# Gate and up products of the experts as three fp32r products, with operands split ahead

## The reference, cut to what matters

```python
h = 512; I = 256; E = 32; TOP_K = 6
def expert_step(acc, inp):
    gu, dn, c = inp
    g = xf @ gu[:I].T
    u = xf @ gu[I:].T
    o = jax.nn.silu(g) * u @ dn.T
    return (acc + c[:, None] * o, None)
routed, _ = jax.lax.scan(expert_step, jnp.zeros_like(xf), (experts_gate_up, experts_down, combine.T))
sh = jax.nn.silu(xf @ shared_gate_w.T) * (xf @ shared_up_w.T)
return (routed + sh @ shared_down_w.T).reshape(b, s, h)
```

## Time and profile before

| | us |
|---|---|
| median of three runs | 1537.28 |
| the profiled execution | 1538.13 |
| its span, first to last instruction | 1536.2 |
| attention stages and feed-forward | about 0 to 1180 |
| routing and shared expert | about 1180 to 1242 |
| loop over 42 expert blocks | about 1249 to 1513 |
| last adds, sums and stores | 1513 to 1536 |
| mean granted TensorE clock | 0.979 |

### The profile page before, as it was taken

How to read it: one execution, slowest core, us unless ns; L and a number is a source line. 1 busy time by engine, 2 the same in 40 slices (tenths; PEclk the granted TensorE clock), 3 DMA queues, 4 the chain that set the end, 5 groups by cost and what they waited for, 6 DMA issues and landing times. The chain is left out here.

```text
span 1536.2 us, 23747 instructions
## 1 busy us (share of the span) xinstructions
PE 1464.4 (95%) x8826; PEld 1191.7 (78%) x8826; DVE 844.1 (55%) x2161; ACT 549.2 (36%) x1022; POOL 565.4 (37%) x276
## 2 busy tenths in 40 slices
PE   5999999999999999999999999788998989999994
PEld 4999999989999999899989999636665445555552
DVE  6455555544586755488655578739402634444442
ACT  3344345344354354443444533522211012222331
POOL 5006006006366604374811554526400124444442
PEclk9999999999999999999999999989997999999997
DMA  5102003013003013002112200350004659999999
GB/s 197 63 4 90 5 4 121 4 62 94 26 5 97 3 71 118 28 4 65 33 48 92 78 1 1 148 249 1 1 0 158 229 179 333 350 331 341 332 338 301
DMA packets 63976, 176.97 MB, mean 115 GB/s; under 512 B 15110, under 2 KB 32006, under 8 KB 54028
## 3 DMA queue, kind: packets, MB, share of 16 engines
q1 hardware_dynamic: 53708, 151.57, 27.7%
q0 software_dynamic: 10176, 24.12, 6.4%
HBM read 156.00 MB, written 19.66 MB: 114 GB/s over the span
## 5 line engine op out<-in xcount | busy, mean ns | idle before, releaser
L65 PE MATMUL ps_x<-wkv_hi,c_hi 128*128 128x256 f32 (+1 forms) x832 | 241.2, 290 | 0.0
L67 PE MATMUL ps_x<-wkv_hi,c_lo 128*128 128x256 f32 (+1 forms) x832 | 234.2, 282 | 0.0
L66 PE MATMUL ps_x<-wkv_lo,c_hi 128*128 128x256 f32 (+1 forms) x832 | 234.2, 281 | 0.0
L294 POOL TENSOR_TENSOR c_hi<-c_raw,ones 128x1608 fp32r<-128x1608 f32 x31 | 90.1, 2905 | 344.8 <-DMA c_raw<-ctxT 344.8
L769 DVE TENSOR_TENSOR pT<-ps_x,pT 128x512 fp32r<-128x512 f32 (+1 forms) x224 | 145.1, 648 | 123.3 <-ACT pT L617 120.6
L65 PE MATMUL ps_x<-c_hi,wkv_hi 128*128 128x402 f32 x512 | 195.7, 382 | 2.9 <-POOL c_lo L297 2.3
L617 ACT CAST pT<-ps_x 128x512 fp32r<-128x512 f32 (+1 forms) x224 | 124.5, 556 | 167.4 <-PE ps_x L472 164.4
L67 PE MATMUL ps_x<-c_hi,wkv_lo 128*128 128x402 f32 x512 | 177.9, 347 | 0.0
L66 PE MATMUL ps_x<-c_lo,wkv_hi 128*128 128x402 f32 x512 | 177.8, 347 | 0.0
L65 PEld LDWEIGHTS ps_x<-wkv_hi,c_hi 128*128 128x128 f32 (+1 forms) x832 | 153.5, 184 | 17.0 <-issue 17.0
L598 ACT CAST vv<-ps_x 128x512 fp32r<-128x512 f32 (+1 forms) x112 | 62.1, 555 | 278.5 <-PE ps_x L67 278.5
(11 more groups left out here) (314 smaller groups left out, 2685.6 us busy)
## 6 DMA issues: line engine op xcount, KB each, us to landing
e_w_gu<-w_gu SPq DMA_DIRECT2D x49, 1024.0 KB, 7.9
c_raw<-ctxT SPq DMA_DIRECT2D x32, 804.0 KB, 5.0
e_w_dn<-w_dn SPq DMA_DIRECT2D x48, 512.0 KB, 5.6
x_tok<-slabs SPq DMA_DIRECT2D x13, 1024.0 KB, 4.8
spare<-slabs SPq DMA_DIRECT2D x8, 1024.0 KB, 11.1
h_late<-slabs SPq DMA_DIRECT2D x4, 1024.0 KB, 16.6
e_mix<-shared SPq DMA_DIRECT2D x2, 1536.0 KB, 8.5
wkv_raw<-w_qkv SPq DMA_DIRECT2D x2, 1024.0 KB, 12.3
```

The costliest lines, as they stand in the source:

```text
L65: nc.tensor.matmul(out, a_hi, b_hi, start=start, stop=False)
L66: nc.tensor.matmul(out, a_hi, b_lo, start=False, stop=False)
L67: return nc.tensor.matmul(out, a_lo, b_hi, start=False, stop=stop)
L294: nc.gpsimd.tensor_tensor(c_hi[:, :, chunk(c)], c_raw[:, :, chunk(c)], ones[:, 0:1].unsqueeze(2).to_broadcast([P, KD, CW]), ALU.mult).then ...
```

## The change

The weights of gate and up are loaded into `gu_raw` as before. ScalarE now rounds them to fp32r (`split_high`, 2048 numbers in each partition, into a ring of three), three blocks ahead. VectorE subtracts to get the low part of three of the four slices (`split_low`, 1536 numbers), GpSimd that of the fourth (512 numbers), both two blocks ahead and in place, over `gu_raw`. The turned block is split too: ScalarE's copy writes its high part and VectorE's `turned_low` (512 numbers from PSUM) the low part. `gate_up` becomes four calls of mm3, twelve fp32r matmuls. `turned` now waits until gate_up of two blocks before is done, as its ring has two places instead of six. `pick_slots` makes its table in one instruction with broadcasts instead of four, into a ring of two. Ahead of the loop, the wait for the tables and the reading of the loop count are moved ahead of shared_down(1), the turns of the first two blocks lie between the shared expert's down products, VectorE makes the first table for the loop before hidden(0), and the first splits lie around them. Two buffers of the shared expert share space with the third place of the high ring.

```diff
-        w_gu = sb("e_w_gu", [P, U, KD, 2 * I])
+        gu_raw = sb("e_gu_raw", [P, U, KD, 2 * I])
+        gu_lo = nc.alloc_sbuf_tensor_at("e_gu_lo", [P, U, KD, 2 * I], F32R, offset=nc.sbuf_base - 4 * U * KD * 2 * I)
+        gu_hi = sb("e_gu_hi", [P, 3, KD, 2 * I], F32R)
+        gu_hi_2 = nc.sbuf_base - 4 * KD * 2 * I
+        assert 4 * T * 4 <= 4 * KD * 2 * I
...
-        pick = sb("e_pick", [P, U, TT, P], F32R)
+        pick = sb("e_pick", [P, 2, TT, P], F32R)
...
-        xT = sb("e_xT", [P, U, D])
+        xT_hi, xT_lo = (sb(f"e_xT_{n}", [P, 2, D], F32R) for n in ("hi", "lo"))
...
-        s_sg, s_t1, s_hid = sb("r_sg", [P, 2, T]), sb("r_t1", [P, 2, T]), sb("r_hid", [P, 2, 2, T])
+        s_sg, s_t1 = (nc.alloc_sbuf_tensor_at(f"r_{n}", [P, 2, T], F32, offset=gu_hi_2 + 8 * T * i) for i, n in enumerate(("sg", "t1")))
+        s_hid = sb("r_hid", [P, 2, 2, T])
...
-        xT_full, xT_done = sem("e_xT_full"), sem("e_xT_done")
+        xT_full, xT_hi_done, xT_lo_done = sem("e_xT_full"), sem("e_xT_hi_done"), sem("e_xT_lo_done")
+        gu_hi_done, gu_lo_done, gu_lo3_done = sem("e_gu_hi_done"), sem("e_gu_lo_done"), sem("e_gu_lo3_done")
...
                     wait_turn(sp, gu_full, nth(i, r, plus=1 - U))
-                sp.dma_start(w_gu[:, r % U], a["w_gu"][e]).then_inc(gu_loaded[r % U], 16)
+                sp.dma_start(gu_raw[:, r % U], a["w_gu"][e]).then_inc(gu_loaded[r % U], 16)
             def down(i, r, first=False):
...
+            def split_low(i, r):
+                wait_turn(pool, gu_hi_done, nth(i, r, plus=1))
+                nc.gpsimd.tensor_tensor(gu_lo[:, r % U, 3], gu_raw[:, r % U, 3], f32(gu_hi[:, r % 3, 3]), ALU.subtract).then_inc(gu_lo3_done, 1)
+
...
             for r in range(AHEAD):
                 gather(0, r)
+                if r >= AHEAD - 2:
+                    split_low(0, r + 2 - AHEAD)
...
             with pool.Fori(0, turns(pool)) as i:
                 for r in range(U):
                     gather(i, r + AHEAD)
+                    split_low(i, r + 2)
                     scatter(i, r)
...
-                if not isinstance(i, int) or r >= U:
-                    dve.wait_ge(info_full, nth(i, r, plus=1 - U))
+                if not isinstance(i, int) or r >= 2:
+                    dve.wait_ge(info_full, nth(i, r, plus=-1))
...
-                for t in range(TT):
-                    ins = nc.vector.tensor_scalar(pick[:, b, t], slot[:, 0:P], rel[:, b, t:t + 1], None, ALU.is_equal)
-                ins.then_inc(pick_done, 1)
+                nc.vector.tensor_tensor(pick[:, r % 2], slot[:, 0:P].unsqueeze(1).to_broadcast([P, TT, P]),
+                                        rel[:, b].unsqueeze(2).to_broadcast([P, TT, P]), ALU.is_equal).then_inc(pick_done, 1)
+
+            def split_low(i, r):
+                dve.wait_ge(gu_hi_done, nth(i, r, plus=1))
+                nc.vector.tensor_tensor(gu_lo[:, r % U, 0:3], gu_raw[:, r % U, 0:3], f32(gu_hi[:, r % 3, 0:3]), ALU.subtract).then_inc(gu_lo_done, 1)
+
+            def turned_low(i, r):
+                dve.wait_ge(xT_hi_done, nth(i, r, plus=1))
+                nc.vector.tensor_tensor(xT_lo[:, r % 2], ps[:, XT], f32(xT_hi[:, r % 2]), ALU.subtract).then_inc(xT_lo_done, 1)
             def rows_in(i, r):
...
             for r in range(AHEAD):
...
+                else:
+                    split_low(0, 0)
                 rows_in(0, r)
...
                     shared_hidden(1 + r // 2)
+            split_low(0, 1)
             for t in range(TT):
...
+                if t in (1, 2):
+                    turned_low(0, t - 1)
+            pick_slots(0, AHEAD)
             hidden(0, 0)
-            pick_slots(0, AHEAD)
             with dve.Fori(0, turns(dve)) as i:
                 for r in range(U):
                     rows_in(i, r + AHEAD)
+                    split_low(i, r + 2)
+                    turned_low(i, r + 2)
...
                     hidden(i, r + 1)
             for t in range(TT):
...
         def _(act):
             def turned(i, r):
...
-                nc.scalar.copy(xT[:, r % U], ps[:, XT]).then_inc(xT_done, 1)
+                if not isinstance(i, int) or r >= 2:
+                    act.wait_ge(gu_full, nth(i, r, plus=-1))
+                nc.scalar.copy(xT_hi[:, r % 2], ps[:, XT]).then_inc(xT_hi_done, 1)
+
+            def split_high(i, r):
+                act.wait_ge(gu_loaded[r % U], landed(i, r))
+                if not isinstance(i, int) or r >= 3:
+                    act.wait_ge(gu_full, nth(i, r, plus=-2))
+                nc.scalar.copy(gu_hi[:, r % 3], gu_raw[:, r % U]).then_inc(gu_hi_done, 1)
             def gates(i, r):
...
+            for r in range(3):
+                if r == 2:
+                    act.wait_ge(s_hid_done, 4)
+                split_high(0, r)
             turned(0, 0)
             turned(0, 1)
             gates(0, 0)
...
                 for r in range(U):
                     turned(i, r + 2)
                     hidden_turned(i, r)
+                    split_high(i, r + 3)
                     gates(i, r + 1)
...
                 for t in range(TT):
-                    ins = nc.tensor.matmul(ps[:, INFO, 0:NF], pick[:, b, t], facts[:, b, t], start=(t == 0), stop=(t == TT - 1))
+                    ins = nc.tensor.matmul(ps[:, INFO, 0:NF], pick[:, r % 2, t], facts[:, b, t], start=(t == 0), stop=(t == TT - 1))
...
             def turn(i, r):
...
-                    pe.wait_ge(xT_done, nth(i, r))
+                    pe.wait_ge(xT_lo_done, nth(i, r))
...
             def gate_up(i, r):
...
-                pe.wait_ge(gu_loaded[b], landed(i, r))
-                pe.wait_ge(xT_done, nth(i, r, plus=1))
+                pe.wait_ge(gu_lo3_done, nth(i, r, plus=1))
+                pe.wait_ge(gu_lo_done, nth(i, r, plus=1))
+                pe.wait_ge(xT_lo_done, nth(i, r, plus=1))
...
-                    ins = nc.tensor.matmul(ps[:, GU], xT[:, b, P * g:P * g + P], w_gu[:, b, g], start=(g == 0), stop=(g == KD - 1))
+                    c = slice(P * g, P * g + P)
+                    ins = mm3(nc, ps[:, GU], xT_hi[:, r % 2, c], xT_lo[:, r % 2, c], gu_hi[:, r % 3, g], gu_lo[:, b, g],
+                              g == 0, g == KD - 1)
...
             def turn_hidden(i, r):
...
                 look_up(0, r)
             shared_down(0)
             look_up(0, AHEAD - 1)
-            for t in range(1, TT):
-                shared_down(t)
+            pe.wait_ge(tables_done, 2)
+            n = turns(pe)
+            shared_down(1)
             turn(0, 0)
+            shared_down(2)
             turn(0, 1)
+            shared_down(3)
...
-            pe.wait_ge(tables_done, 2)
-            n = turns(pe)
             with pe.Fori(0, n) as i:
                 for r in range(U):
                     look_up(i, r + AHEAD)
```

## The result

The changed kernel takes 1514.55 us (median of 4 runs, 1512.40 to 1515.61); the kernel before took 1537.74 us beside it (4 runs). The ratio is 0.9848, 95% interval 0.9836 to 0.9860. The profiled execution took 1515.2 us with a span of 1513.1 us, against a span of 1536.2 us before: 23.1 us less.

What follows compares the result with a forecast made beforehand. TensorE was taken to bound the loop at 6.23 us per block, the DMA engines close behind. Entry 4.9 us plus 41 x (6.23 - 5.95) = 11.5 us gave 16.4 us: 1521 us from the median of 1537.28, range 1504 to 1541 us.

Steps and rivals of the forecast that it cites:

- the case that made the forecast: Loop: DMA engines or a light lock set a block of 5.8 to 6.2 us, 1515 to 1532 us; chance 0.54.
- Products: gate_up on TensorE: twelve fp32r matmuls, 2.76 to 2.84 us, replace 3.44 us; TensorE's block falls to 5.55 to 5.63 us.
- ScalarE: Loop: one added rounding of 1.90 us brings ScalarE to 3.8 us per block, hidden with 0.2 us to spare.
- VectorE: Loop: with split_low, turned_low and the one-instruction table, VectorE needs 5.4 us per block beside TensorE's 5.6.
- the lock: Loop: VectorE waits a whole 1.27 us GpSimd instruction per block, block 6.67 us, 1550 us; chance 0.15.
- GpSimd: Loop: with a 1.27 us split added, scatter, gather and split take 4.8 to 5.5 us per block and fit, barely.
- DMA pace: Loop: the DMA engines need 5.95 us to move a block's 2.1 MB, taken for all blocks.
- the signs that I named for this pace: Loop profile: gate_up waits for a split while ScalarE waits for weights, landings grow past 12 us, rate over 360 GB/s.
- Entry: Ahead of the loop: gate_up(2) waits for GpSimd's third split until 1255.4 us, saving 4.9 us; bounds 2 and 8.5 us.
- End: Behind the last block: unused loads queue ahead of the final reads of the sums, so the end follows DMA pace.
- TensorE's pace: Loop: TensorE sets a block of 5.60 us and the DMA engines have room, 31 us gained, 1507 us; chance 0.25.

Runs made afterwards that it cites:

- two products: The changed kernel with the product of low turned block by high weights left out of gate_up, all splits still made: 1512.07 us (1 run).
- three ahead: The changed kernel with GpSimd's split made three blocks ahead instead of two, one more split at the entry: 1526.20 us.
- the operand from PSUM: The changed kernel with VectorE's split in the loop taking its first input from PSUM, so one SBUF input instead of two: 1539.67 us.
- two slices: The changed kernel with GpSimd splitting two of the four slices and VectorE the other two: 1537.21 us (1 run).
- single products: Gate and up from one product of rounded weights by rounded turned block, no low parts made by any engine: 1502.59 us.
- the vector splits: The changed kernel with VectorE making the low part of all four slices and GpSimd none: 1506.58 us; once more, 1507.00 us.

## Why the prediction was right, and where it was off

The time lay in the range, and it moved the way that was forecast; the gain was 22.7 us from the median where 16.3 were forecast. Part of that is luck. The loop gained 20.9 us where 11.5 were forecast, and entry and end gave 1.5 and 1.2 us less than forecast. Its block of 5.70 us lies outside the 5.8 to 6.2 us of the case that made the forecast, and the cause was not the one named. By its own steps:

- **Products.** 12 x 0.23 us, and the free block at the entry is 5.59 us: inside 5.55 to 5.63. Right, and the removed cost was all there to be had.
- **ScalarE.** Hidden: it never appears in front of TensorE.
- **VectorE.** 5.4 us of work per block were forecast; it is busy 33.68 of 40 us, or 4.8 us per block of 5.70, the single terms as taken (1.76, 0.68, 0.69 us). It met the lock after all: lightly in the changed kernel (a mean of 1.82 instead of 1.76 us for its split), and by 0.6 to 1.5 us a block in four experiments (two products, three ahead, the operand from PSUM, two slices).
- **GpSimd.** 4.8 to 5.5 us in order "fits, barely". This is the step that failed. The sum was near: 1.29 + 2.38 + 1.00 + 0.30 + 0.02 + at least 0.17 (the least wait ahead of a scatter, as with two products) is 5.2 us. But the prediction took the scatter at the 1.58 us of the kernel before, and it takes 2.30 us beside VectorE's split; and it added up the engine's work without following who waits at either end of it. VectorE's split waits for GpSimd's, the scatter for VectorE's, and the next split stands behind the scatter. That circle closes at 5.69 us, above TensorE's 5.59.
- **DMA pace.** 5.95 us was the term that made the forecast. It was somewhat too long, and it was wrongly let stand for all blocks. With single products, where ScalarE waits for the weights, the engines set 5.70 to 5.75 us. The loop with the vector splits ran at 5.59 us, faster than that, for all its 40 blocks without a wait for weights, and lived on the slack of the deep prefetch: from issue to landing its 1 MB loads took 10.8 us at the loop's start and 16.8 us at its end. DMA view of that kernel, 1255 to 1290 and 1450 to 1490 us:

```profile
e_gu_raw<-w_gu SPq DMA_DIRECT2D x6, 1024.0 KB, 10.8
...
e_gu_raw<-w_gu SPq DMA_DIRECT2D x6, 1024.0 KB, 16.8
```

6.0 us over some 35 blocks is 0.17 us a block, an estimate of 5.76 us for the engines' pace that agrees with the single products. At 5.95 us the slack of 9 us would have been gone after 25 blocks, as the prediction said; at 5.76 it outlasts the 42. Of the signs that I named for this pace, the rate over 360 GB/s came in the changed kernel, and the landings past 12 us in the one with the vector splits, but ScalarE did not wait for the weights in either. The changed kernel's rows don't give its landings. That the loop came out slower than TensorE was right; the reason was another. The share of 1.02 rose to 1.05 with 8% more bytes per us, so it had not said that there was no room.

- The Trainium skill (DMA: Bandwidth & Descriptors, Specifications) has 358 GB/s for a core's HBM; the loop with the vector splits moved 367 GB/s over 40 us, so the measurement decides here too.
- **Entry.** gate_up(2) was forecast at 1255.4 us behind GpSimd's split; it came at 1255.81. The split fell between two bounds, though: the clock was lost as well, so the entry saved 3.4 us, not 4.9. At the second down product, counted from the stage's start, the order of the entry is worth 6.9 us on the kernel before, nothing with GpSimd's split, and 6.7 us without it: an edit's worth depends on what is late next.
- **End.** I let it stand as it was. It grew by 1.2 us, and by 3.0 to 3.3 us with the vector splits. From the chain that ended last, the last scatter's way to HBM and the last read of the sums, in the kernel before, the changed one, and the first with vector splits:

```profile
1516.17 8.37 DMA acc<-e_mix,e_row_out
1527.98 5.10 DMA e_mix<-acc
...
1491.90 9.19 DMA acc<-e_mix,e_row_out
1504.53 5.36 DMA e_mix<-acc
...
1482.04 9.48 DMA acc<-e_mix,e_row_out
1494.95 7.24 DMA e_mix<-acc
```

These two stretches are 1.1 us and 3.25 us longer, which is nearly all of the growth. The loads of blocks past the last stand in the queue ahead of the reads of the sums, as the prediction said, and the fuller queue would make them late. That this queue is the reason was argued from these rows; no run leaves the unused loads out.

- **Rivals.** TensorE's pace would have been 1507 us: it is what the vector splits gave. The lock as forecast (VectorE waiting a whole GpSimd instruction once per block, 1550 us) did not come in the changed kernel, but with one PSUM operand it gave 1539.67 us and with the split three ahead 1526.20 us. It came in the changed kernel in a form I had not weighed: GpSimd is the one that waits, 0.7 to 0.8 us in every scatter, and VectorE hardly at all. The trace of the kernel before had both sides. VectorE's product of the earlier trace rows had not waited for a whole instruction, but for the rest of the one that ran (until 1087.10, and it ended 1.08 us later), and GpSimd's next product was then the slow one:

```profile
1084.76 2.34 POOL L1140 TENSOR_TENSOR h_prod<-t_att,t_v 128x1024 f32<-128x1024 f32 x1
1087.07 3.34 POOL L1140 TENSOR_TENSOR h_prod<-t_att,t_v 128x1024 f32<-128x1024 f32 x1
```

The sum as measured: 3.4 + 40 x 0.52 - 1.2 = 23 us of span.

## What to carry to other kernels

When an engine off the critical path gets work for which the critical one will wait, add up not only its own work but every closed path on which it lies: from an instruction, over all that it waits for and that holds it, back to the same instruction, divided by the blocks between. A path can be closed by two side engines that hold each other, and then it has its own pace whatever the critical engine does. Here that circle was 0.1 us longer than TensorE's block. Giving the same work to VectorE, the engine with the heavier load, took GpSimd's split out of it and gained 8 us between the medians. In the profiles, from the stage's start, that is 7 us at the entry and 4.6 us in the loop, less 2 us at the end. If two paths come out equally long, as the circle and the ring did here, shorten something that lies on one of them alone before you name the cause. And before VectorE and GpSimd both get subtractions of SBUF operands, write down which instruction of the one will lie beside which of the other; a tiny one can stand for as long as the other's whole instruction.

## What the runs showed of the hardware

- A VectorE operation with two SBUF inputs holds back GpSimd's issue of an indirect DMA until it ends: scatter 2.3 to 2.9 us beside a subtraction, 1.58 us alone or beside the same operation with one input from PSUM. Its end follows VectorE's and not its own start: it started 0.8 to 1.5 us before the subtraction's end in four kernels and ended 1.45 to 1.47 us after it. A gather of 1.00 us took 2.41 us in the same place (three blocks ahead). The Trainium skill (SBUF — State Buffer, Who interferes with whom) says that such an operation contends with a GpSimd instruction that reads SBUF, and infers that it leaves the making of an indirect DMA's descriptors alone, which VectorE's two-port modes hold up; here the plain subtraction held scatter and gather, so the measurement goes further than the rule.
- The other way round VectorE waits until GpSimd's instruction ends, whatever its own size. The subtraction of 1536 numbers, 1.76 us alone, took up to 2.75 us and ended 1.63 us after GpSimd's split, whenever it had started. Four numbers took 1.69 to 1.87 us beside GpSimd's split of 1.28 us, and ended within 0.06 us of its end; their record begins 0.4 to 0.6 us before that of the split, and why is open.
- An fp32r product 128 x 128 x 512 takes 0.23 us where the fp32 one took 0.86 (3.44 / 4), so the three products of four chunks cost 2.8 us where fp32 costs 3.44.
- In the mix of weights and indirect DMAs one core moved 362 to 367 GB/s over 40 us at share 1.05, with the weights waited for or not; 338 at 1.02 was not its limit.
